# Differential attention on one core: the row maxima turned by DMA instead of by VectorE

## The reference, cut to what matters

```python
scores = jnp.einsum('bhqd,bhkd->bhqk', q, k)          # 16 batches x 32 half heads x 1024 x 1024
probs = jax.nn.softmax(scores.astype(jnp.float32), axis=-1)
probs = probs.reshape(b, H, 2, s, s)
w = probs[:, :, 0] - lam * probs[:, :, 1]
attn = jnp.einsum('bhqk,bhkd->bhqd', w, v)             # then RMS norm, gain, and Wo
```

## Time and profile before

| | |
|---|---|
| median of 3 runs | 6063.33 us (6057.4 to 6066.57) |
| the profiled execution, its own time | 6064.04 us |
| its span | 6062.2 us |
| busy: PE, DVE, ACT, POOL | 5630.7, 5537.9, 4845.1, 2006.0 us |
| mean granted TensorE clock | 0.97 of full speed |
| DMA queue of SP: packets, share of 16 engines | 435171, 32.7% |

### The profile page before, as it was taken

One profiled execution on the slowest core, in us unless ns is written; L12 is line 12 of the kernel. 1 busy time (PEld: TensorE's weight loads), 2 busy tenths in 40 slices (PEclk: granted clock), 3 DMA queues, 4 the chain that ended last, 5 costly groups with the idle time before them and its releaser, 6 DMA issues. The chain is left out here.

```text
span 6062.2 us, 166095 instructions
## 1 busy us (share of the span) xinstructions
PE 5630.7 (93%) x50896; PEld 2015.1 (33%) x50896; DVE 5537.9 (91%) x6200; ACT 4845.1 (80%) x8950; POOL 2006.0 (33%) x3781
## 2 busy tenths in 40 slices
PE   8878999999999999999999999999999999987775
PEld 4542233333333333333333333333233323325424
DVE  7868999999999999999999999999999999967706
ACT  5755888888888888889888888888888888873304
POOL 7981222222222222222222222222222222225406
PEclk9997999999999999999999999999999999998877
DMA  5672222222232222222222222222222222216598
GB/s 178 203 202 49 49 52 52 51 52 52 52 52 51 52 51 52 51 50 52 52 47 51 52 51 48 51 51 51 50 52 52 52 52 51 52 35 199 173 359 272
DMA packets 436840, 493.13 MB, mean 81 GB/s; under 512 B 99283, under 2 KB 298099, under 8 KB 436195
## 3 DMA queue, kind: packets, MB, share of 16 engines
q1 hardware_dynamic: 435171, 483.57, 32.7%
q10 hardware_dynamic: 1024, 0.53, 0.0%
HBM read 360.60 MB, written 123.21 MB: 80 GB/s over the span
## 5 line engine op out<-in xcount | busy, mean ns | idle before, releaser
L677 ACT ACTIVATE at_e<-at_ps_e 128x512 f32<-128x512 f32 x8192 | 4368.8, 595 | 542.5 <-PE at_ps_e L766 373.2
L691 DVE TENSOR_REDUCE at_largest<-at_ps_m 128x1 f32<-128x1024 f32 x4096 | 4671.1, 1202 | 56.2 <-PE at_ps_m L795 53.0
L782 PE MATMUL at_ps_o<-at_e,at_v 128*32 128x256 f32 (+1 forms) x30720 | 2687.1, 422 | 12.3 <-issue 8.2
L795 PE MATMUL at_ps_m<-k_stack,q_stack 48*128 48x512 bf16 x8192 | 2500.1, 385 | 132.7 <-DVE at_largest L691 58.3
L766 PE MATMUL at_ps_e<-q_stack,k_stack 51*128 51x512 bf16 x8192 | 2505.7, 383 | 5.2 <-issue 2.3
L782 PEld LDWEIGHTS at_ps_o<-at_e,at_v 128*32 128x32 f32 x30720 | 845.0, 149 | 1567.3 <-issue 935.0
L766 PEld LDWEIGHTS at_ps_e<-q_stack,k_stack 51*128 51x128 bf16 x8192 | 598.1, 93 | 1678.3 <-ACT at_e L677 1641.0
L596 POOL TENSOR_TENSOR at_negated<-at_zeros,at_largest_t 128x32 f32<-128x32 f32 x256 | 64.7, 253 | 3262.7 <-DVE at_largest_t L698 3262.7
L795 PEld LDWEIGHTS at_ps_m<-k_stack,q_stack 48*128 48x128 bf16 x8192 | 607.6, 93 | 203.5 <-DVE at_largest L691 172.2
L639 POOL TENSOR_TENSOR at_rms<-at_mean_eps,at_minus_half 128x16 f32<-128x16 f32 x128 | 372.7, 2912 | 10.0
L436 PE MATMUL pr_ps_q<-pr_xn_t,pr_w 128*128 128x512 f32 x512 | 232.3, 596 | 2.0 <-issue 1.3
(11 more groups left out here) (130 smaller groups left out, 2856.0 us busy)
## 6 DMA issues: line engine op xcount, KB each, us to landing
k_stack<-k_parts SPq DMA_DIRECT2D x1536, 64.0 KB
q_stack<-q_parts SPq DMA_DIRECT2D x256, 192.0 KB
q_stack<-q_parts SPq DMA_DIRECT2D x256, 128.0 KB
w_first<-in_w SPq DMA_DIRECT2D x32, 1024.0 KB, 11.7
ex_w_second<-in_w SPq DMA_DIRECT2D x32, 1024.0 KB, 12.7
q_parts<-pr_parts SPq DMA_DIRECT2D x96, 256.0 KB, 2.4
k_parts<-pr_parts SPq DMA_DIRECT2D x96, 256.0 KB, 2.8
pr_x_in<-in_x SPq DMA_DIRECT2D x16, 1024.0 KB, 5.8
```

Source lines behind the costliest of these rows:

```text
L677: nc.scalar.activation(e[:, j % E_BUFS], ps_e[:, bank(u, j)], ACT.Exp, scale=SCALE).then_inc(exp_done, 1)
L691: nc.vector.reduce_max(largest[:, u % 2, j // SIDE, j % SIDE:j % SIDE + 1], ps_m[:, j % 2], AX.X).then_inc(max_done, 1)
L782: last = nc.tensor.matmul(ps_o[32 * tile:32 * tile + 32, columns], v[:, u, tile // 2, kt::TILES], e[:, (QUAD * g + tile) % E_BUFS, columns ...
L795: last = nc.tensor.matmul(ps_m[:, j % 2, half * HALF:(half + 1) * HALF], q_stack[rows, u, pair, c, t * P:(t + 1) * P], k_stack[rows, u, pa ...
```

## The change: what it does

The maxima leave DVE's stream of work after the reduction. `largest` now has 16 columns. `load_rows` on SP waits for the reductions themselves, stores `largest` as it is to DRAM (L544 of the changed kernel, [128 queries x 16 tiles] in f32, 64 bytes per partition), waits for it to land, and loads it back with tile and query exchanged (L549) into `largest_t` [16 x 128]. Neighbouring elements of a row of `largest_t` lie 64 bytes apart in DRAM, so the load names 2048 single elements of 4 bytes. POOL's `split` has its five instructions as before, on [16 x 128] instead of [128 x 32], and waits for that load. Since `parts` then holds 8 tiles of a matrix on 8 partitions, six DMAs from SBUF to SBUF (L554) write the rows of `q_stack` directly, where one DMA from DRAM stood before. DVE loses the 256 transposes, a memset, and gains a wait for the load of two quads earlier before it overwrites `largest`.

```diff
-        self.max_scr = scratch("max_parts", (b * QKH // 2, PARTS, 2, S), BF16)
+        self.max_scr = scratch("maxima", (b * QKH // 2, P, 2 * TILES), F32)
...
-            largest, largest_t = sb("largest", [P, 2, 2, BLK]), sb("largest_t", [P, BLK])
-            zeros, negated, rest = sb("zeros", [P, BLK]), sb("negated", [P, BLK]), sb("rest", [P, BLK])
-            parts = sb("parts", [P, PARTS, BLK], BF16)
+            largest, largest_t = sb("largest", [P, 2, 2, SIDE]), sb("largest_t", [SIDE, P])
+            zeros, negated, rest = sb("zeros", [SIDE, P]), sb("negated", [SIDE, P]), sb("rest", [SIDE, P])
+            parts = sb("parts", [SIDE, PARTS, P], BF16)
...
                 def load_rows(n, u, c):
+                    sp.wait_ge(max_done, TRIES * n + SIDE * (c + 1) + 2)
+                    maxima = self.max_scr[bass.ds(2 * n + c, 1)]
+                    sp.dma_start(maxima.rearrange("o q t -> (o q) t"), largest[:, u % 2, c]).then_inc(max_stored, 16)
+                    sp.wait_ge(max_stored, 16 * (2 * n + c + 1))
+                    if not (isinstance(n, int) and n == 0 and c == 0):
+                        sp.wait_ge(split_done, 2 * n + c)
+                    with nc.allow_non_contiguous_dma(reason="maxima, one element per query and tile"):
+                        sp.dma_start(largest_t[:], maxima.rearrange("o q t -> (o t) q")).then_inc(max_turned, 16)
                     sp.wait_ge(split_done, 2 * n + c + 1)
-                    maxima = self.max_scr[bass.ds(2 * n + c, 1)]
-                    by_block = maxima.rearrange("o r pair (t g q) -> g (o pair t) r q", t=TILES, q=BLK)
-                    for g in range(P // BLK):
-                        sp.dma_start(by_block[g], parts[BLK * g:BLK * g + SIDE]).then_inc(max_stored, 16)
-                    sp.wait_ge(max_stored, 16 * (P // BLK) * (2 * n + c + 1))
-                    row = SCORE_ROW + PRODUCTS
-                    sp.dma_start(q_stack[row:row + PARTS, u, :, c], maxima.rearrange("o r pair s -> (o r) pair s")).then_inc(
-                        rows_loaded[c][u], 16)
+                    for r in range(PARTS):
+                        row = SCORE_ROW + PRODUCTS + r
+                        for pair in range(PAIR):
+                            sp.dma_start(q_stack[row:row + 1, u, pair, c], parts[TILES * pair:TILES * (pair + 1), r]).then_inc(
+                                rows_loaded[c][u], 16)
...
                 def maximum(m, u, j):
+                    if j % SIDE == 0:
+                        dve.wait_ge(max_turned, 16 * (2 * (m - 2) + j // SIDE + 1 + TURNS_BEFORE))
                     dve.wait_ge(tries_done, TRIES * m + j + 1)
                     nc.vector.reduce_max(largest[:, u % 2, j // SIDE, j % SIDE:j % SIDE + 1], ps_m[:, j % 2], AX.X).then_inc(max_done, 1)
-
-                def turn_maxima(m, u, c):
-
-                    dve.wait_ge(max_done, TRIES * m + SIDE * (c + 1) + 2)
-                    if not (isinstance(m, int) and m == 0 and c == 0):
-                        dve.wait_ge(split_done, 2 * m + c)
-                    nc.vector.transpose(largest_t[:], largest[:, u % 2, c]).then_inc(max_turned, 1)
```

More of the change, by code:

```diff
@@ L478, in attend @@
         loops = quads // BUFS - 1
-        PE_HEAD, ACT_HEAD, DVE_HEAD = 200, 160, 176
+        PE_HEAD, ACT_HEAD, DVE_HEAD = 200, 160, 196
         with ExitStack() as ctx:
@@ L517, in attend @@
             ONES = 4
+            TURNS_BEFORE = 4
+            ROW_DMAS = PARTS * PAIR
             SPLIT_STEPS, FINISH_STEPS = 4, 14
@@ L591, in _, with split @@
                 pool.wait_ge(ones_set, ONES)
-                def split(h, base):
-                    pool.wait_ge(max_turned, h + 1)
+                def split(h, base, i, u, c):
+                    pool.wait_ge(max_turned, 16 * (h + 1 + TURNS_BEFORE))
                     nc.gpsimd.tensor_tensor(negated[:], zeros[:], largest_t[:], ALU.subtract).then_inc(pool_step, 1)
-                    if not (isinstance(h, int) and h == 0):
-                        pool.wait_ge(max_stored, 16 * (P // BLK) * h)
+                    if c == 1:
+                        pool.wait_ge(rows_loaded[0][u], 16 * ROW_DMAS * (i + 1))
+                    elif not (isinstance(h, int) and h == 0):
+                        pool.wait_ge(rows_loaded[1][(u - 1) % BUFS], 16 * ROW_DMAS * (i + (u > 0)))
                     nc.gpsimd.tensor_tensor(parts[:, 0], zeros[:], largest_t[:], ALU.subtract).then_inc(pool_step, 1)
@@ L645, in finish, with turn @@
                                             ALU.mult).then_inc(attn_done, 1)
-                def turn(n, rows, base):
+                def turn(i, u, rows, base):
+                    n = BUFS * i + u
                     if rows:
                         for c in range(2):
-                            split(2 * (n + AHEAD) + c, base)
+                            split(2 * (n + AHEAD) + c, base, i + (u + AHEAD) // BUFS, (u + AHEAD) % BUFS, c)
                             base = base + SPLIT_STEPS
@@ L654, in _ @@
                 for h in range(2 * AHEAD):
-                    split(h, SPLIT_STEPS * h)
+                    split(h, SPLIT_STEPS * h, 0, h // 2, h % 2)
                 pool.wait_ge(lam_done, 1)
@@ L659, in _ @@
                     for u in range(BUFS):
-                        turn(BUFS * i + u, True, start + steps * (BUFS * i + u))
+                        turn(i, u, True, start + steps * (BUFS * i + u))
                 for u in range(BUFS):
                     n = BUFS * loops + u
-                    turn(n, u < BUFS - AHEAD, start + steps * n - 2 * SPLIT_STEPS * max(0, u - (BUFS - AHEAD)))
+                    turn(loops, u, u < BUFS - AHEAD, start + steps * n - 2 * SPLIT_STEPS * max(0, u - (BUFS - AHEAD)))
             @block.scalar
@@ L681, in _ @@
             def _(dve):
-                nc.vector.memset(largest[:], 0.0).then_inc(largest_set, 1)
-                dve.wait_ge(largest_set, 1)
                 dve.sem_inc(max_done, 2)
+                dve.sem_inc(max_turned, 16 * TURNS_BEFORE)
                 dve.sem_inc(sums_read, 1)
@@ L708, in turn_out, with period @@
                     nc.vector.transpose(out[:, u % 2], attn_t[:].rearrange("p b s v -> p (b s v)")).then_inc(out_done, 1)
-                def period(n, u, g, tries, rows=True, last_quad=True, this_quad=True):
+                def period(n, u, g, tries, last_quad=True, this_quad=True):
                     if tries:
                         maximum(n + AHEAD, u + AHEAD, 2 * g)
[L713 to L716, removed]
                     if g == LAG - 1 and last_quad:
@@ L740, in _, with turn @@
                 for g in range(HEAD):
-                    period(0, 0, g, True, rows=False, last_quad=False)
-                def turn(n, u, tries, next_tries, rows):
+                    period(0, 0, g, True, last_quad=False)
+                def turn(n, u, tries, next_tries):
                     for g in range(HEAD, GROUPS):
-                        period(n, u, g, tries, rows)
+                        period(n, u, g, tries)
                     for g in range(HEAD):
-                        period(n + 1, u + 1, g, next_tries, rows)
+                        period(n + 1, u + 1, g, next_tries)
                 with hinted(nc, dve, 0, loops, slot=DVE_HEAD) as i:
                     for u in range(BUFS):
-                        turn(BUFS * i + u, u, True, True, True)
+                        turn(BUFS * i + u, u, True, True)
                 for u in range(BUFS):
-                    turn(BUFS * loops + u, u, u < BUFS - AHEAD, u + 1 < BUFS - AHEAD, u < BUFS - AHEAD)
+                    turn(BUFS * loops + u, u, u < BUFS - AHEAD, u + 1 < BUFS - AHEAD)
             @block.tensor
@@ L806, in period @@
                     if g % TILES == 0 and this_quad:
-                        pe.wait_ge(rows_loaded[g // TILES][u], 16 * (i + 1))
+                        pe.wait_ge(rows_loaded[g // TILES][u], 16 * ROW_DMAS * (i + 1))
                     if g == 0 and tries:
```

4 lines of the change are left out of this document (1 added, 3 removed).

## The result

The changed kernel takes 6630.93 us (median of 4 runs, 6601.28 to 6642.83) against 6061.75 us before (median of 4 runs, one more than in the table ahead of the prediction): ratio 1.0931, 95% interval 1.0894 to 1.0969. It is 9.3% slower; forecast were 6450 us and a range of 6035 to 7590. The profiled execution took 6628.28 us, span 6626.4.

What follows compares the result with a forecast made beforehand. DVE was taken as the bound at 38.4 us a quad; SP's chain, 30.7 + 2 G with G = 5.4, made 41.5, so 3.1 more over 124 turns, 384 us on 6064: 6450 us, range 6035 to 7590.

Steps and rivals of the forecast that it cites:

- The removed work: On DVE: 256 transposes of the maxima, each costing 0.10 us of its stream, 26 us in all.
- G: On SP: time from issue of the new load L549 to its landing, twice a quad, taken as 5.4 us.
- The six row DMAs: On SP, per side: issuing the six DMAs that write the stacks' rows, taken as 2.3 us.
- The first stack load to side 0's load: On SP: from the first stack load until side 0's maxima store has landed, taken as 18.1 us.
- the gap ahead of the next side 1: On SP: the load of v and its gaps before side 1 comes again, taken as 0.7 us.
- the store to its landing: On SP: the store of side 1's `largest` to DRAM, one DMA, taken as 1.4 us to landing.
- split and wakes: Per side: POOL's wake and five split instructions, 2.6 us, then SP's wake, 0.16 us.
- the formula 30.7 + 2 G: SP's serial chain per quad in us, hidden under DVE's 38.4 as long as G is below 3.9.
- the third rival: On SP: row DMAs cost 0.79 us each, 5 us a quad, 620 us, giving 7070 us; chance 0.1.
- the threshold: SP's chain is hidden while under DVE's 38.4 us a quad, G below 3.9 us, some late quads aside.
- The lower bound: For G: v's load landing after 2.1 us plus 1.0 for 112 more packets of 9.0 ns, 3.1 us.
- the second rival: In load L549: single-element reads queue up at DRAM, G above 10 us, 7590 us at G = 10; chance 0.17.

Runs made afterwards that it cites:

- e1: Changed kernel with the load of the maxima reading the same 8 KB as 16 contiguous runs of 512 bytes instead of single elements: 6242.87 us.
- e7: Changed kernel with SP's instructions reordered: nine of the 18 stack loads issued during the wait for side 1's maxima and split: 6093.95 us.
- e4: Kernel before the change without DVE's transposes of the maxima, only their signal kept and the split working on zeros: 6034.06 us.
- e2: Changed kernel with rows written the old way, one store to DRAM and one load, in place of six row DMAs a side: 6359.46 us.
- e6: Changed kernel with the sides outermost in the stacks, so three row DMAs a side instead of six: 6269.75 us.
- e11: Changed kernel with three row DMAs a side and interleaved stack loads, plus side 0's load of the maxima done twice: 6163.75 us.
- e10: Changed kernel with three row DMAs a side and interleaved stack loads, plus side 1's load of the maxima done twice: 6498.90 us.

## Why the prediction was right

**The bound and the place.** DVE's stream, SP's serial chain and two loads in it per quad were right: the idle time moved to PE's wait for rows, SP's rows follow each other with 1.1 us a quad of waiting for DVE in them, e1 took 3.0 us off the quad for 2.0 us off each of its two loads, and e7 removed nearly all of the loss by order alone.

**The removed work.** 26 us, confirmed by e4 (25.5). In the changed kernel they are not on the path.

**The sum's terms.** Forecast 41.5 us a quad, measured 43.0. Two terms were each off by more than that total. G was taken as 5.4 and is 3.6 to 3.7: 3.5 us too much in a quad. The six row DMAs were taken as 2.3 us and are 4.1: 3.6 too little. They cancel. The first stack load to side 0's load was taken as 18.1 and is 18.6, the gap ahead of the next side 1 as 0.7 and is 1.8, the store to its landing as 1.4 and is 1.7; split and wakes came out 0.2 to 0.3 us a side shorter than taken. With 43.0 the sum is 6064 + 124 x 4.6 = 6634 us, against 6628.28 of the profiled execution.

**What was luck.** With the measured G and the row issues of 2.3, the formula 30.7 + 2 G gives 38.1, which the prediction's rule calls hidden: the answer would have been 6038. The prediction named the sign itself: a median landing of L549 under 3.9 us would make it wrong to the fast side. The landing was 3.6, and the kernel was slower all the same. So the forecast "slower" stood on a G that was too dear, and its coming true is luck. Two things that its sum did not hold made up for it. One is the price of the row DMAs, the third rival: it had 0.79 us each and a chance of 0.1, and 0.69 from issue to issue was measured. The other is the threshold.

**The threshold.** The prediction held a chain under 38.4 us to be hidden, but for some late quads. That was too sharp. Without SP's waits for DVE (slack above 0.7) the chain of e1 is 37.5 us, of e2 38.3 and of e6 37.5, and still a quad took 40.0, 40.8 and 40.1 us, and the runs were 181, 298 and 208 us above the kernel before. e6 has the G of the changed kernel and cheaper rows than the sum had (1.9 us a side), so even with its own row price the sum would not have been hidden. The prediction let the attention stores wait for POOL's finish only; it left out that DVE reaches its transpose of the output late when PE started the quad late. That this path is what holds these runs back fits the table of e11 and is not shown by a run of its own.

**Where G went wrong.** I chose the store of `v_tiles` as the nearest row because it has as many runs. Its time more likely goes with its 1 MB, which no run tests. The single elements cost an engine no more than the 64-byte packets did; this is the DMA queue of the changed kernel from 2526.5 to 2529.5 us, behind the load issued at 2525.61:

```profile
q1 hardware_dynamic: 2064, 0.01, 38.8%
```

0.388 x 16 x 3 us / 2064 = 9.0 ns each. The 2064 are the 2048 elements and 16 more. The lower bound, built from just that, was 3.1; where the missing 0.5 us lies no run shows. The slow reads of the second rival did not occur. The Trainium skill, DMA: Bandwidth & Descriptors (Bandwidth), with its 10.5 ns per packet, gave an estimate of 3.2 and so the better G; the trace shows 9.0 ns. The conclusion that the prediction drew from that estimate, no stall, would still have been wrong, since the dear row DMAs were not in it.

**The covers.** That POOL's finish was covered held while SP was the bound: in the changed kernel DVE waits for it 3 times, 22.0 us in all. Its threshold (12.8 + G against 17.6) was half a microsecond too generous, as e10 showed. That PE's lower clock costs nothing was argued from the chain, and no run tests it. In the changed kernel the stretch from side 0's last row issue to the next transpose of the output takes 22.3 us on average and 20.4 at least; how much of that difference is the clock stays open.

## What to carry to other kernels

Before work is moved to a queue that issues in order, add up that queue's whole cycle, issue times and every wait for a landing included, and compare it with the bound: here 0.2 us of vector work a quad was given away for a quad that is 4.6 us longer. Leave some microseconds of room: chains that added up to 0.1 to 0.9 us less than the bound still cost 181 to 298 us. Where such a chain must be, put independent issues into its waits; the same DMAs in another order gave back 537 of 569 us. A DMA costs its issuer per instruction (here 0.64 us with 2 KB and 0.59 with 4 KB), and one shape can cost twice another (0.28 for a stack load), so count instructions before elements.

## What I had not expected of the hardware

A load of 2048 single elements of 4 bytes, 64 bytes apart in DRAM, lands after 3.6 us, only 2.0 us more than the same 8 KB in 16 runs (1.6 us), at 9.0 ns of an engine for each packet. The load of 32 bytes per partition from a single address had run at 114 packets per us; this one passes 1809 of its 2064 in the microsecond from 2527.0 to 2528.0, so that row's pace is not one of small reads in general. And the issue of a row DMA from 8 or 16 partitions to one partition takes SP 0.64 and 0.59 us, where the stack loads take 0.28 (k_stack, medians).
